# Gated cross attention: the product of the rows with their inverse norms goes from VectorE to ScalarE and GpSimd, and three queues get another order

## The reference, cut to what matters

```python
def _L0_xattn_ref(q, k, v, Wq, Wk, Wv, Wo, bo, g):     # b = 32, DIM = 64, 8 heads of 64, n = 512
    qh, kh, vh = (einsum('bcn,oc->bon', t, W).reshape(b, 8, 64, n) ...)
    qh = softmax(qh, axis=-2) * SCALE
    kh = softmax(kh, axis=-1)
    context = einsum('bhdn,bhen->bhde', kh, vh)
    out = einsum('bhde,bhdn->bhen', context, qh).reshape(b, 512, n)
    out = einsum('bcn,oc->bon', out, Wo) + bo[None, :, None]
    norm = maximum(sqrt(sum(out * out, axis=1, keepdims=True)), 1e-12)
    return out / norm * g * sqrt(64)

x = x + tanh(g_xattn) * _L0_xattn_ref(_layernorm(x), ctx, ctx, ...)
x = x + tanh(g_ffn) * _L0_ffn_ref(_layernorm(x), ...)   # gated FFN with 4-bit weights, 512 -> 1376 -> 512
```

## Time and profile before

| | |
|---|---|
| median of 3 runs | 686.31 us (685.57 to 686.65) |
| the profiled execution's own time | 685.41 us |
| its span, first to last instruction | 683.6 us |
| TensorE's mean granted clock | 0.993 |
| busy: PE | 655.9 us (96%) |
| busy: DVE | 588.5 us (86%) |
| busy: ACT | 467.9 us (68%) |
| busy: POOL | 382.2 us (56%) |
| chain of waits that ended last | PE 77%, DVE 9%, ACT 4%, issue 4%, POOL 3%, DMA 2% |
| attention, up to the drain's origin | 386.5 us of the span |

### The profile page before, as it was taken

One profiled execution on the slowest core, in us unless ns is written; L12 is line 12 of the kernel. 1 busy time (PEld: TensorE's weight loads), 2 busy tenths in 40 slices (PEclk: granted clock), 3 DMA queues, 4 the chain that ended last, 5 costly groups with the idle time before them and its releaser, 6 DMA issues.

```text
span 683.6 us, 14565 instructions
## 1 busy us (share of the span) xinstructions
PE 655.9 (96%) x5141; PEld 343.6 (50%) x5141; DVE 588.5 (86%) x785; ACT 467.9 (68%) x822; POOL 382.2 (56%) x448
## 2 busy tenths in 40 slices
PE   7899999999999999999999988999999999999995
PEld 6454555455455545545554533445444544454443
DVE  7677889989898988888888578999999999988987
ACT  4787677667767767776776746667766765666663
POOL 6212433433442443334246297798788877887886
PEclk8999999999999999999999999999999999999999
DMA  4112312412322221122111100000010001000102
GB/s 116 36 38 69 94 40 69 102 44 63 93 76 54 68 83 33 57 76 75 40 52 26 26 6 2 1 1 2 0 40 23 1 1 47 17 1 16 47 0 63
DMA packets 32047, 28.98 MB, mean 42 GB/s; under 512 B 20047, under 2 KB 22234, under 8 KB 32002
## 3 DMA queue, kind: packets, MB, share of 16 engines
q1 hardware_dynamic: 29594, 27.73, 14.7%
q10 hardware_dynamic: 2408, 0.70, 0.4%
HBM read 22.42 MB, written 4.23 MB: 39 GB/s over the span
## 4 chain that ended last, share of the span: by engine, by line
PE 77%; DVE 9%; ACT 4%; issue 4%; POOL 3%; DMA 2%; SPq 1%; DVEq 0%; POOLq 0%
PE pair L1418 8%; PE small_pair L1124 7%; PE pair L1419 7%; PE pair L1205 6%; PE small_pair L1093 6%; PE pair L1079 5%; PE pair L1442 4%; PE pair L1454 4%; PE small_pair L1418 4%; PE small_pair L1108 4%; PE small_pair L1419 4%; PE pair L1058 3%; ACT eq L721 3%; PE pair L1237 2%; DVE eq L1685 2%
## 5 line engine op out<-in xcount | busy, mean ns | idle before, releaser
L1815 DVE SCALAR_TENSOR_TENSOR acc<-pair,scale_T,acc 128x512 f32<-128x512 f32 (+1 forms) x176 | 131.7, 749 | 15.5 <-ACT acc L868 2.3
L712 ACT ACTIVATE ek<-pair,kneg 128x512 f32<-128x512 f32 x128 | 86.6, 683 | 35.0 <-DVE kneg L1680 34.9
L621 POOL TENSOR_TENSOR yT<-yT,y_scaled 128x512 f32<-128x512 f32 (+1 forms) x78 | 100.5, 1290 | 4.7 <-ACT y_scaled L893 3.9
L1685 DVE TENSOR_TENSOR eq<-eq,pair 128x1024 f32<-128x1024 f32 x64 | 77.8, 1216 | 24.0 <-PE pair L1188 24.0
L1675 DVE TENSOR_REDUCE qmax<-pair 128x16 f32<-128x1024 f32 x64 | 78.0, 1219 | 17.3 <-PE pair L1058 17.3
L1418 PE MATMUL pair<-ek,w_gu 128*128 128x512 f16 (+1 forms) x235 | 91.3, 389 | 1.5 <-DVE acc L1815 1.2
L1419 PE MATMUL pair<-ekT,w_gu 128*128 128x512 f16 (+1 forms) x235 | 89.1, 379 | 0.0
L721 ACT ACTIVATE eq<-pair 128x1024 f32<-128x1024 f32 x64 | 65.7, 1026 | 23.1 <-PE pair L1215 23.0
L1680 DVE TENSOR_REDUCE kneg<-pair 128x2 f32<-128x1024 f32 x64 | 77.8, 1216 | 3.1 <-PE pair L1079 3.0
L1442 PE MATMUL pair<-in_hi,d_int 128*128 128x512 f32 (+1 forms) x132 | 75.7, 575 | 1.3 <-DVE yT L1854 1.3
L599 POOL TENSOR_TENSOR inter<-act_gate,acc 128x512 f32<-128x512 f32 (+1 forms) x43 | 55.2, 1283 | 38.7 <-issue 15.3
(11 more groups left out here) (206 smaller groups left out, 1463.0 us busy)
## 6 DMA issues: line engine op xcount, KB each, us to landing
xall<-in_x SPq DMA_DIRECT2D x16, 256.0 KB, 2.7
ctx_raw<-in_ctx SPq DMA_DIRECT2D x16, 256.0 KB, 2.8
out_x<-xall SPq DMA_DIRECT2D x16, 256.0 KB, 2.0
zero<-zeros_plus SPq DMA_DIRECT2D x8, 344.0 KB, 3.9
packed<-in_L_ffn_gate_qweight SPq DMA_DIRECT2D x4, 688.0 KB
packed<-in_L_ffn_up_qweight SPq DMA_DIRECT2D x4, 688.0 KB
packed<-in_L_ffn_down_qweight SPq DMA_DIRECT2D x10, 256.0 KB
zero<-zeros_plus SPq DMA_DIRECT2D x5, 256.0 KB, 3.8
```

The lines of the kernel that those rows point to most:

```text
L621: pool.tensor_tensor(yT16[:, nt, :] if it == IT - 1 else total, total, y_scaled[:, nt, :], ALU.add).then_inc(z_add, 1)
L712: act.activation(ek[:, b, t, :], k_pairs[t % 2][:, b, :], ACT.Exp, bias=kneg[:, b, t:t + 1], scale=-1.0, accum_out=ksum[:, k_slot(b, t):k_ ...
L1685: dve.tensor_tensor(e, e, dve_pair[:, :, :], ALU.mult).then_inc(q_norm, 1)
L1815: dve.scalar_tensor_tensor(out=acc[0:w, n % 2, m, :], in0=gu_bank[(8 * n + job) % 3][0:w, :], scalar=scale_T[0:w, it, 4 * m + g:4 * m + g ...
```

## The change

- `normed_and_gated(p-3)` leaves VectorE's steps 3 to 16 (14 calls); the two for pairs 14 and 15, inside the FFN, stay.
- ScalarE gets `inverse_norms`: it copies the spread inverse norms from PSUM, times the gate, into `yn`. GpSimd gets `normed`: `yn = yn * y0`, ahead of `residual_added`. TensorE's `output(0)` waits for ScalarE's copy instead of VectorE's product; ScalarE's `outputs` waits until GpSimd has read `y0`.
- VectorE's order: `reciprocals` ahead of `layernorm_apply`; `normalise(1)` ahead of `folded`; `context_rows` last.
- TensorE's order: `ctx_transposed` behind `less_max(3)` instead of ahead of `spread_reciprocals(3)`.

```diff
@@ gpsimd
+            def normed(k):
+                pool.wait_ge(rn_evac, k + 1)
+                pool.wait_ge(y_evac, 2 * k + 2)
+                pool.tensor_tensor(yn[:, :], yn[:, :], y0[:, :], ALU.mult).then_inc(yn_ready, 1)
+
...
                     layernorm(p + 1)
                     if residual and at_least(p, 3):
+                        normed(p - 3)
                         residual_added(p - 3)
...
             step(PAIRS - 1, 1, True, False)
+            normed(PAIRS - 3)
             residual_added(PAIRS - 3)
@@ scalar
+                def inverse_norms():
+                    if not at_least(p, 3):
+                        return
+                    act.wait_ge(rn_mm, p - 2)
+                    if at_least(p, 4):
+                        act.wait_ge(x1_done, p - 3)
+                    act.activation(yn[:, :], small[1][:, :], ACT.Copy, scale=gate_col[:, 0:1]).then_inc(rn_evac, 1)
+
                 def outputs():
                     act.wait_ge(f_mm, r)
+                    if combine and at_least(p, 3):
+                        act.wait_ge(yn_ready, p - 2)
...
                 denominators()
                 k_transposed(3, back=1)
+                inverse_norms()
                 k_exps(0)
@@ tensor
                         if at_least(p, 3):
-                            pe.wait_ge(yn_ready, r - 1)
+                            pe.wait_ge(rn_evac, r - 1)
...
                 spread_reciprocals(2)
                 q_logits(2)
                 less_max(2)
-                ctx_transposed()
                 spread_reciprocals(3)
                 q_logits(3)
                 less_max(3)
+                ctx_transposed()
                 k_transposed(2)
@@ vector
-                    if at_least(p, 3):
-                        normed_and_gated(p - 3)
                     k_maxima(0)
                     q_maxima(1)
                     k_maxima(1)
+                    reciprocals()
                     if not last:
                         layernorm_apply(p + 1)
-                    reciprocals()
                     q_maxima(2)
...
                 normalise(0)
                 bound_norms(r2)
+                normalise(1)
                 folded()
-                normalise(1)
                 normalise(2)
-                context_rows()
                 if last:
                     less_zero(p, *weights, 0)
                 normalise(3)
                 key_sums()
+                context_rows()
```

More of the change, by code:

```diff
@@ L231, in layer @@
             sem(n) for n in ("t_max", "k_max", "k_exp", "k_done", "kt_evac", "q_exp", "q_norm"))
-        d_mm, a_mm, m_mm, qmaxT_mm, ct_mm, f_mm, ss_mm = (
-            sem(n) for n in ("d_mm", "a_mm", "m_mm", "qmaxT_mm", "ct_mm", "f_mm", "ss_mm"))
+        d_mm, a_mm, m_mm, qmaxT_mm, ct_mm, f_mm, ss_mm, rn_evac = (
+            sem(n) for n in ("d_mm", "a_mm", "m_mm", "qmaxT_mm", "ct_mm", "f_mm", "ss_mm", "rn_evac"))
         d_evac, a_evac, m_evac, qmaxT_evac, ct_evac, y_evac, ss_evac = (
```

## The result

The changed kernel takes **730.38 us** (median of 4 runs, 729.87 to 731.56) against 686.32 for the kernel before beside it (685.57 to 686.65). The ratio is 1.0646 (95% interval 1.0628 to 1.0664). It is slower, as forecast, but by 44 us and not by 24: the forecast of 710 us and its range of 697 to 718 are missed. Of the profiled execution the span is 729.8 us (before: 683.6), the mean granted clock of TensorE 0.960 (before: 0.993).

A forecast was written before the change was run, and what follows sets the result against it. TensorE sets the step, with the load and `xn` at the edge: steps 3 to 14 lose 22.0 us, the drain 1.9, together 24, giving 710 us on the median of 686.3; range 697 to 718.

The forecast's parts named there:

- What bounds the kernel: Steps 3 to 10: TensorE nearly gapless; load, VectorE's front part and `xn` already at the edge of making it wait.
- The late load, 1.4 us: Context load waits for the moved transposes; each step's statistics start about 2.65 us after the origin instead of 1.25.
- The transposes' own 0.15 us a step: TensorE: last query logits no longer stand behind the context transposes, saving 0.15 us a step, bounds 0 and 0.24.
- The product off VectorE, 0.7: VectorE's queue ahead of `xn` gets about 0.7 us shorter, as the product took 0.74.
- the reciprocals ahead of `xn`, 1.0: On VectorE, putting the reciprocals first makes `xn` 1.0 us later.
- The collision, 0.8: GpSimd's residual sum holds VectorE's cast of the reciprocals, making `xn` 0.8 us later; bounds 0 and 1.27.
- ScalarE's copy with the gate, 0: A 0.69 us copy ending before TensorE's output group: cost 0, up to 0.3 a step without the 0.26 cover.
- The step = (start of `xn`) + 2.59 + 13.61 - 0.15: Step length: 2.59 us from `xn` to fourth key logits, 13.61 to next origin; 26.0 in steps 3 to 10.
- The drain, 1.9: Behind the last origin, GpSimd's sum starts 1.9 us later, on the chain to the inverse norms; bounds 0 and 1.9.
- "Their being earlier earns nothing": Reciprocals ahead of `xn`: what they feed is wanted only late in the step, so being earlier gains nothing.

The follow-up runs named there:

- g5_all: The changed kernel with early load of x, `xn` ahead of the reciprocals, GpSimd's residual sum later, the drain's product back on VectorE: 680.2 us.
- g1_x_early: The changed kernel with the load of x issued early under its own semaphore, the context's load left late: 691.9 us.
- b1: The kernel before with early load of x under its own semaphore, and late context transposes and context rows: 683.2 us.
- b3: Also b3_norm_first: b1 with the normalised rows of tile 1 ahead of the fold on VectorE: 681.4 us.
- f3_recip_back: The changed kernel with `xn` ahead of the reciprocals on VectorE again, context transposes left late: 699.4 us.
- k1_sum_later: g1_x_early with GpSimd's residual sum moved behind its low part of `xn`: 688.4 us.
- f1_fill: The changed kernel with matmuls by zeros between TensorE's third and fourth key-logit groups, from step 2 on: 715.9 us.
- h1_drain: The changed kernel with context transposes and reciprocals at their old places, and the drain's product back on VectorE: 686.1 us.
- f2_ctx_back: The changed kernel with context transposes back ahead of the fourth spread reciprocals on TensorE, reciprocals left ahead of `xn`: 696.9 us.

## Why the prediction was wrong in size and right in kind

- *What bounds the kernel*: right. TensorE sets the step, and `xn` is the edge; "(start of `xn`) + 2.59" held in step 9 to the hundredth (251.93 to 254.52). It is an edge on one side only: with `xn` at 7.01 (g5_all) the fourth key logits start 10.06 after the origin, as they do with `xn` at 7.47.
- *The late load, 1.4 us*: right. Statistics at 2.3 to 2.87 after the origin, forecast 2.65. g1_x_early, which takes only this away, gives back 38 us of the 44; a good part of that is the clock that goes with it. The Trainium skill's fit that the prediction set beside its row ("DMA: Bandwidth & Descriptors", section "Anatomy of one DMA — SWDGE (gpsimd) path") is given for DMAs that GpSimd issues, and this load is SyncE's; in the kernel after it landed 2.8 us after its issue in the median, as in the row.
- *The transposes' own 0.15 us a step*: the size is right, the cause half right; b1 and b3 show that VectorE's order of rows and fold is the other half.
- *The product off VectorE, 0.7; the reciprocals ahead of `xn`, 1.0*: right for the late statistics of the change. From their start to `xn` step 9 took 6.22 us before and 5.56 in f3_recip_back, which has the product gone and `xn` first: 0.66. With early statistics the product is worth only 0.27 (`xn` at 7.28 in b3_norm_first, 7.01 in g5_all), and nothing in steps 11 to 14, where `xn` starts at 7.01 with it and without. The reciprocals cost 0.94: `xn` starts at 7.95 with them first (k1_sum_later) and at 7.01 behind `xn` (g5_all).
- *The collision, 0.8*: right. The cast took 0.89 to 1.19 us in steps 3 to 14, 0.20 where the sum was moved away. The Trainium skill ("SBUF — State Buffer", the section on who interferes with whom) lets whoever issued first block the other for its whole instruction; every held cast here ended with the sum, which agrees, and by the worst case of that rule the price would have been 1.27.
- *ScalarE's copy with the gate, 0*: right. TensorE's output group starts 4.59 after the origin, as before.
- *The step = (start of `xn`) + 2.59 + 13.61 - 0.15*: **here it failed**. 13.46 is what step 3 took (13.49) and what f1_fill took everywhere. With TensorE idle for 1.9 to 2.8 us ahead of it, and the clock low around the end of that wait, steps 4 to 14 took 14.85 to 16.29. The forecast had this number from step 5 of the kernel before, where the wait was short and the clock full, and carried it over to waits several times as long. At full clock steps 1 to 15 lose 41.1 - 18.1 = 23.0 us, forecast 22.0; the 18.1 had no term and no rival. That they hang on the wait is shown by f1_fill, not only argued. That the sum for the full clock came so near is not luck in the main, since its parts were right one by one.
- *The drain, 1.9*: right for the chain, too low for the price. The sum comes 5.70 after the origin (forecast 5.65). The matmul that waits for the inverse norms comes 28.83 after it (458.23 against 429.40), where before it came 26.91 after it (413.40 against 386.49): 1.9 later, as forecast. But the change paid 3.2 us. Of the eight kernels with the product on GpSimd in the drain, four had 3.4 us at half clock there and paid 1.7, four had 6.8 and paid 3.2 to 3.3, behind waits of 2.71 to 2.76 us in all of them. So the 1.3 over the forecast go with the longer half clock. All of it vanishes with the product's return (h1_drain).
- *"Their being earlier earns nothing"* of the reciprocals: f3_recip_back shows that too simple. With `xn` first, cast and subtraction meet GpSimd's sum and low part behind it and hold the maxima, and half of what the early `xn` gains is lost there. So the 13.61 was not fixed either: in steps 4, 6 and 8 of the kernel before, whose subtraction was held for 1.3 us, that part had taken 14.18 to 14.25.

The half-clock stretches of steps 4 to 14 add up to 41 us (ten of 3.41 and one of 6.83). The Trainium skill ("TensorE: Matmul & The Clock Gate", section "HAM oscillation — how this bites in real kernels") describes a kernel in which a wait on every tile brings the low clock back on every tile, and counts half of the throttled time as lost: by it an estimated 20.5 us here. The trace agrees with the mechanism and nearly with the figure: the rows give 18.0 for these steps, less among other things because six of the stretches begin while TensorE still waits, 0.1 to 0.8 us ahead of its next matmul. The Trainium skill puts the waits of that kernel at 3 to 5 us; here 1.87 to 2.79 were enough in eleven steps of twelve. A rival with such a stretch in most of the twelve steps, at the 18 us that they took, would have lain near 728 us.

## What to carry to other kernels

Where a gapless TensorE gets a new wait in every step, price it twice: the wait, and the work behind it at half clock; a trace without such waits can't show the second. Here waits of 1.87 to 2.79 us brought it in eleven steps of twelve, and those of f2_ctx_back, up to 1.55, in none. Before moving work off an engine, look whether that engine sets the step: here the product's 0.7 us bought under 1 us in the whole kernel, while the orders moved along with it cost 42.5. A load that only a buffer's last reader holds back should not hold back another that has its own place: splitting x from the context was worth 38 us to the change and 2.4 us to the kernel before, together with the late transposes.

## What the runs showed of the hardware that was not expected

- Idle time can make the work behind it dearer: filling the 2.4 us wait of step 9, and its like in the other steps, with 2.37 us of useless matmuls each took 12.4 us off steps 1 to 15.
- Equal waits did not always lower the clock. In the change a wait of 1.89 us in step 3 left it at 2.4 GHz, one of 1.87 in step 14 was followed by 3.4 us at 1.2 GHz; in f2_ctx_back 1.55 us in step 5 left it; in f3_recip_back two waits of 0.78 and 0.63 in step 6 did not, two of 0.79 and 0.60 in step 9 did. What else decides stays open here.
- The low stretches were 3.41 us or twice that. The longer ones came behind TensorE's longest waits (2.71 us in step 6, 2.75 in the drain) but not behind all such: 2.79 us in step 8 was followed by one of 3.41, as was 2.76 in the drain of g1_x_early.
- The first stretch at half clock, at the start of the program, was 3.4, 6.8 or 10.2 us long and followed no edit, and the first origin lay between 28.6 and 30.7 us. Differences of that size between two single profiles say nothing.
